# Two transformer passes: looped layers with phases, against one written-out pipeline with Wv and Wo joined

## The reference, cut to what matters

```python
for i in range(DEPTH):                      # 6
    x = attn_layer(shift_tokens(x), Wqkv[i], q_scale[i], k_scale[i], Wo[i]) + x
    x = ffn_layer(shift_tokens(x), ln_g[i], ln_b[i], W1[i], b1[i], W2[i], b2[i]) + x
```

## Time and profile before

| | us |
|---|---|
| median of three runs | 7947.51 (7939.41 to 7956.17) |
| span of the profiled execution | 7947.7 |
| TensorE busy (matmul) | 6508.3, 82% |
| DVE busy | 5680.7, 71% |
| ScalarE busy | 2813.2, 35% |
| GpSimd busy | 1991.7, 25% |

### The profile page before, as it was taken

The page is one execution under the profiler, slowest core; times in us unless marked ns, Lnnn a source line. Parts: engine busy times, 40 slices in busy tenths (PEclk is TensorE's granted clock), DMA queues, the critical chain, the costliest instruction groups (busy, mean ns, idle before and its releaser), DMA issues. The chain is left out here.

```text
span 7947.7 us, 238408 instructions
## 1 busy us (share of the span) xinstructions
PE 6508.3 (82%) x89716; PEld 4710.8 (59%) x89716; DVE 5680.7 (71%) x26551; ACT 2813.2 (35%) x7328; POOL 1991.7 (25%) x2075
## 2 busy tenths in 40 slices
PE   8999999999976666666666666679999999999887
PEld 5656656565656565655656565656565655656544
DVE  6676767676767777777777777777666676767566
ACT  4444444444432222222222222234444444444311
POOL 4343535353510000000000000034444353535200
PEclk9999999999975555555555555589999999999898
DMA  0000000000000000000000000000000000000000
GB/s 28 11 4 14 1 14 1 14 1 14 1 15 2 2 2 2 2 2 2 2 2 2 2 2 2 2 4 0 15 11 4 11 4 14 1 14 1 18 2 12
DMA packets 30765, 50.49 MB, mean 6 GB/s; under 512 B 2032, under 2 KB 25291, under 8 KB 28235
## 3 DMA queue, kind: packets, MB, share of 16 engines
q1 hardware_dynamic: 29614, 40.54, 1.6%
q10 hardware_dynamic: 412, 0.42, 0.0%
HBM read 39.91 MB, written 1.05 MB: 5 GB/s over the span
## 5 line engine op out<-in xcount | busy, mean ns | idle before, releaser
L1048 PE MATMUL g_bank<-hbuf,Wgates 128*128 128x2 f32 x2048 | 600.9, 363 | 1024.2 <-DVE hbuf L1136 970.3
L1048 PEld LDWEIGHTS g_bank<-hbuf,Wgates 128*128 128x128 f32 x2048 | 513.0, 311 | 1140.0 <-DVE hbuf L1136 1085.3
L1090 ACT ACTIVATE tg<-g_bank 128x2 f32<-128x2 f32 x1024 | 176.1, 172 | 1690.9 <-PE g_bank L1048 1690.9
L1156 POOL TENSOR_TENSOR xB<-hbuf,xA 128x32 f32 x64 | 16.4, 256 | 2853.0 <-DVE hbuf L1136 2853.0
L371 POOL TENSOR_TENSOR t1b<-t1b,t2b 128x1024 f32<-128x1024 f32 x192 | 451.7, 2354 | 687.1 <-DVE t2b L523 687.1
L371 POOL TENSOR_TENSOR t1a<-t1a,t2a 128x1024 f32<-128x1024 f32 x192 | 451.7, 2354 | 684.7 <-DVE t2a L523 684.7
L1060 PE MATMUL e_bank<-tg,Weg 128*128 128x2 f32 x2048 | 579.4, 352 | 0.0
L1032 PEld LDWEIGHTS s_bank<-hparts,Wparts 128*128 128x128 bf16 x12288 | 571.0, 117 | 0.0
L1110 DVE TENSOR_SCALAR sg<-es 128x4 f32<-128x4 f32 x1024 | 174.4, 170 | 554.5 <-ACT es L1092 554.5
L1060 PEld LDWEIGHTS e_bank<-tg,Weg 128*128 128x128 f32 x2048 | 515.1, 312 | 0.0
L1032 PE MATMUL s_bank<-hparts,Wparts 128*128 128x2 bf16 x12288 | 469.6, 165 | 0.0
(11 more groups left out here) (435 smaller groups left out, 16401.7 us busy)
## 6 DMA issues: line engine op xcount, KB each, us to landing
Wqkv<-in_L_ffn_Wqkv SPq DMA_DIRECT2D x13, 1536.0 KB, 6.5
Wo<-in_L_ffn_Wo SPq DMA_DIRECT2D x13, 512.0 KB, 7.6
W<-in_L_ffn_W SPq DMA_DIRECT2D x12, 341.0 KB
W<-in_L_ffn_W SPq DMA_DIRECT2D x12, 128.0 KB
xt<-in_L_attn_x SPq DMA_DIRECT2D x2, 512.0 KB
rope<-in_rope SPq DMA_DIRECT2D x1, 1024.0 KB, 7.5
out<-ot SPq DMA_DIRECT2D x4, 256.0 KB
W<-in_L_ffn_W SPq DMA_DIRECT2D x12, 42.5 KB
```

Source lines behind the costliest of these rows:

```text
L1048: pe.matmul(g_bank[j][:, s * B:(s + 1) * B], Wg[:, 3, 1, :], h, start=False, stop=True, skip_group_check=True).then_inc(g_done, 1)
L1090: act.activation(tg[:, :], g_bank[j][:, s * B:(s + 1) * B], ACT.Tanh).then_inc(tg_ready, 1)
```

## The change

layer_phase and FeedForward go. transformer now builds one program for each engine for all 96 tiles of a pass (six layers of 16), written out, with no loop on the device and no pause between layers. A tile passes through four iterations: project (new), turn and score (now), values and weighting (old; last). The feed-forward part runs in the same iterations, on groups of two tiles (256 tokens), spread over an even and an odd iteration.

- Wv and Wo are joined: for each head the product of its part of Wv and its part of Wo is a 128 x 128 matrix, made on TensorE once for a layer (turn_weights, join_weights, take_weights, keep_weights) during the layer before. The values of a head are then already 128 outputs wide, and the weighting (attend) sums over the heads into one 128 x 128 result; L440, L459, L593 and the copies L623 go, one transpose (turn_output) and a small copy (take_output) come.
- q and k share one pair of banks one after the other: project_k waits until DVE has read q, project_q of the next tile until it has read k. Values and turned probabilities share one bank (vp), the weighted output has one, feed-forward has two.
- Values take 16 matmuls a tile (32-column weights, 512 columns, four column groups); scores and weighting 32 matmuls each with 128-row, 32-column weights over 128 columns. The keys lie in KT with zeros in the rows of the other head.
- DVE subtracts the maximum in two halves of 512 columns, ScalarE takes one exponential over 1024 columns, DVE sums the rows over two axes; GpSimd multiplies the probabilities by the reciprocals (norm_probs, two halves) before they are turned.
- GpSimd also makes the rotation tables and moves the last 32 keys to the next tile's buffer (move_k).
- The statistics of the feed-forward part are made for every two tiles, with the twelve root steps each time (normalise).
- SyncE loads the weights of two layers ahead into double buffers; the first layer's weights are no longer loaded in load_phase but at the start of the pass.

```diff
-def layer_phase(nc, c, layer, nm):
...
+    def project_q(n):
+        layer = tile_place(n)[0]
+        pe.wait_ge(s.weights_in[layer % 2], 16 * (layer // 2 + 1))
+        pe.wait_ge(s.xq_ready, 2 * n + 2)
+        if n:
+            pe.wait_ge(s.k_prod, 2 * n)
+        for h in range(2):
+            last = pe.matmul(qk[h], c.xq[n % 4][:, :], c.Wqk[layer % 2][:, h * 512:(h + 1) * 512], start=True, stop=True)
+        last.then_inc(s.q_done, 1)
+    def project_k(n):
+        layer = tile_place(n)[0]
+        pe.wait_ge(s.q_prod, 2 * n + 2)
+        for h in range(2):
+            last = pe.matmul(qk[h], c.xq[n % 4][:, :], c.Wqk[layer % 2][:, INNER + h * 512:INNER + (h + 1) * 512], start=True, stop=True)
+        last.then_inc(s.k_done, 1)
...
+    def turn_q(n):
+        pe.wait_ge(s.q_scaled, n + 1)
+        if n:
+            pe.wait_ge(s.centred, 2 * n)
+        for half in range(2):
+            for k in range(half * HALF, (half + 1) * HALF):
+                last = pe.transpose(sc[:, k * P:(k + 1) * P], t1[:, k * P:(k + 1) * P], c.ident[:, :])
+            last.then_inc(s.q_turned, 1)
...
+    def score(n):
+            pe.matmul(sc[:, h * 512:(h + 1) * 512], c.identb[:, :], c.mask[:, t, :].unsqueeze(1).to_broadcast([P, 8, KEYS]),
+                      start=True, stop=False, skip_group_check=True)
+        for pair in range(PAIRS):
+            for w in range(NW):
+                last = pe.matmul(sc[WIN * w:WIN * w + WIN, pair * 2 * KEYS:(pair + 1) * 2 * KEYS],
+                                 c.QT[:, pair, WIN * w:WIN * w + WIN],
+                                 c.KT[n % 2][:, pair, :, WIN * w:WIN * w + KEYS],
+                                 start=False, stop=True, skip_group_check=True)
+        last.then_inc(s.scored, 1)
...
+    def values(n, w):
+        layer = tile_place(n)[0]
+        pe.wait_ge(s.wvo_ready, 4 * (layer + 1))
+        if w == 0 and n:
+            pe.wait_ge(s.v_ready, 4 * n)
+            before, j = divmod(n + 1, TILES)
+            if before + 1 < N // TILES and 6 <= j < 8:
+                pe.wait_ge(s.wv_ready, 2 * (before + 1) + j - 5)
+            if before + 1 < N // TILES and 8 <= j < 12:
+                pe.wait_ge(s.wvo_ready, 4 * (before + 1) + j - 7)
+        if w == 1 or w == 3:
+            pe.wait_ge(s.v_ready, 4 * n + w)
+        if w == 2:
+            pe.wait_ge(s.pt_ready, 2 * n + 2)
+        for hq in range(4):
+            last = pe.matmul(vp[WIN * hq:WIN * hq + WIN, :], c.xq[n % 4][:, WIN * w:WIN * w + WIN], c.Wvo[layer % 2][:, hq, :],
+                             start=True, stop=True)
+        last.then_inc(s.v_done, 1)
...
+    def attend(n):
+        pe.wait_ge(s.v_ready, 4 * n + 4)
+        pe.wait_ge(s.pt_ready, 2 * n + 2)
+        if n:
+            pe.wait_ge(s.x_done, n)
+        first = NW * (n % 2)
+        for pc in range(2):
+            for quad in range(QUADS):
+                for w in range(NW):
+                    slot = (first + w - 1 + pc) % (2 * NW)
+                    last = pe.matmul(o[WIN * w:WIN * w + WIN, 0:P], c.PT[:, pc, quad * P + WIN * w:quad * P + WIN * w + WIN],
+                                     c.Vw[:, slot, quad * P:(quad + 1) * P],
+                                     start=(pc == 0 and quad == 0), stop=(pc == 1 and quad == QUADS - 1), skip_group_check=True)
+        last.then_inc(s.pv_done, 1)
...
+    def join_weights(layer, hq):
+        pe.wait_ge(s.wv_ready, 2 * layer + 2)
+        if hq:
+            pe.wait_ge(s.wvo_ready, 4 * layer + hq)
+        par = hq % 2
+        rows = slice(64 * par, 64 * par + 64)
+        for quad in range(QUADS):
+            pair = 2 * quad + hq // 2
+            last = pe.matmul(vp[:, quad * P:(quad + 1) * P], c.WvT[rows, pair, :], c.Wo[rows, pair, :], start=True, stop=True)
+        last.then_inc(s.wvo_done, 1)
...
+    for i in range(N + 6):
+        new, now, old, last = i, i - 1, i - 2, i - 3
+        even, g = i % 2 == 0, (i - 4) // 2
+        layer, j = divmod(i, TILES)
+        if new < N:
+            project_q(new)
+        if 0 <= now < N:
+            turn_q(now)
+        if 0 <= last < N:
+            attend(last)
+        if 0 <= old < N:
+            values(old, 0)
+        if 0 <= now < N:
+            turn_k(now)
+        if 0 <= last < N:
+            turn_output(last)
+        if 0 <= old < N:
+            values(old, 1)
+        if even and 0 <= g - 1 < G:
+            lins(g - 1)
+        if not even and 0 <= g < G:
+            back(g)
+        if new < N:
+            project_k(new)
+        if 0 <= old < N:
+            turn_probs(old, 0)
+        if 0 <= now < N:
+            score(now)
+        if 0 <= old < N:
+            turn_probs(old, 1)
+            values(old, 2)
+        if even and 0 <= g - 1 < G:
+            contract(g - 1)
+        if not even and 0 <= g < G:
+            gates(g)
+        if 0 <= old < N:
+            values(old, 3)
+        if even and 0 <= g < G:
+            rows(g)
+        if layer + 1 < N // TILES and 6 <= j < 12:
+            pe.wait_ge(s.v_ready, 4 * (old + 1))
+            if j < 8:
+                turn_weights(layer + 1, j - 6)
+            else:
+                join_weights(layer + 1, j - 8)
...
+    def rotate_q(n):
+        dve.wait_ge(s.table, 4 * (tile_place(n)[0] + 1))
+        dve.wait_ge(s.q_sq, n + 1)
+        if n:
+            dve.wait_ge(s.q_turned, 2 * n)
+            dve.wait_ge(s.q_sum, n)
+        rotate(0, n, s.q_prod)
+    def rotate_k(n):
+        dve.wait_ge(s.k_sq, n + 1)
+        if n:
+            dve.wait_ge(s.k_turned, 2 * n)
+            dve.wait_ge(s.k_sum, n)
+        rotate(1, n, s.k_prod)
...
+    def norms(n):
+        dve.wait_ge(s.q_ssq, n + 1)
+        dve.wait_ge(s.k_ssq, n + 1)
+        if n:
+            dve.wait_ge(s.q_scaled, n)
+            dve.wait_ge(s.k_scaled, n)
+        rsqrt_steps(dve, s.newton, n * NEWTON, c.ssq[:, :], c.rnorm[:, :], c.ntmp[:, :], 1e-24, 0.0)
+    def largest(n):
+        dve.wait_ge(s.scored, n + 1)
+        dve.tensor_reduce(c.mx[:, :], sc.rearrange("p (h j) -> p h j", j=KEYS), AX.X, ALU.max).then_inc(s.max_done, 1)
+        dve.wait_ge(s.max_done, n + 1)
+        if n >= 2:
+            dve.wait_ge(s.p_turned, 2 * (n - 1))
+        for pc in range(2):
+            dve.tensor_tensor(c.probs[n % 2][:, :, pc, :, :],
+                              sc.rearrange("p (q h a j) -> p q h a j", h=4, a=2, j=WIN)[:, :, :, pc, :],
+                              c.mx[:, :].rearrange("p (q h) -> p q h", h=4).unsqueeze(3).to_broadcast([P, QUADS, 4, WIN]),
+                              ALU.subtract).then_inc(s.centred, 1)
+    def row_sums(n):
+        dve.wait_ge(s.exp_done, n + 1)
+        if n >= 2:
+            dve.wait_ge(s.inverted, n - 1)
+        dve.tensor_reduce(c.rsum[n % 2][:, :].rearrange("p (q h) -> p q h", h=4),
+                          c.probs[n % 2][:, :, :, :, :].rearrange("p q a h j -> p q h a j"), AX.XY, ALU.add).then_inc(s.summed, 1)
+    def invert(n):
+        dve.wait_ge(s.summed, n + 1)
+        if n >= 2:
+            dve.wait_ge(s.p_scaled, 2 * (n - 1))
+        dve.reciprocal(c.rinv[n % 2][:, :], c.rsum[n % 2][:, :]).then_inc(s.inverted, 1)
...
+    for i in range(N + 6):
+        new, now, old, last = i, i - 1, i - 2, i - 3
+        even, g = i % 2 == 0, (i - 4) // 2
+        if new < N:
+            rotate_q(new)
+            squares_q(new)
+        if 0 <= last < N:
+            residual(last)
+        if even and 0 <= g - 1 < G:
+            multiply(g - 1)
+        if new < N:
+            rotate_k(new)
+        if 0 <= now < N:
+            largest(now)
+        if even and 0 <= g - 1 < G:
+            finish(g - 1)
+        if new < N:
+            squares_k(new)
+            norms(new)
+        if 0 <= now < N:
+            row_sums(now)
+            invert(now)
+        if even and 0 <= g < G:
+            normalise(g)
...
+    def exponent(n):
+        act.wait_ge(s.centred, 2 * n + 2)
+        pr = c.probs[n % 2][:, :, :, :, :].rearrange("p q a h j -> p (q a h j)")
+        act.activation(pr, pr, ACT.Exp).then_inc(s.exp_done, 1)
...
+    def move_k(n):
+        if n:
+            pool.wait_ge(s.kt_ready, 4 * n)
+        if n >= 2:
+            pool.wait_ge(s.scored, n - 1)
+        for par in range(2):
+            rows = slice(64 * par, 64 * par + 64)
+            if n % NT == 0:
+                pool.memset(c.KT[n % 2][rows, :, par, 0:WIN], 0.0).then_inc(s.k_moved, 1)
+            else:
+                pool.tensor_copy(c.KT[n % 2][rows, :, par, 0:WIN], c.KT[1 - n % 2][rows, :, par, P:]).then_inc(s.k_moved, 1)
+            pool.wait_ge(s.k_moved, 2 * n + par + 1)
+    def add_q(n):
+        pool.wait_ge(s.q_prod, 2 * n + 2)
+        pool.tensor_tensor(t1[:, 0:INNER], t1[:, 0:INNER], t2[:, 0:INNER], ALU.add).then_inc(s.q_sum, 1)
+    def add_k(n):
+        pool.wait_ge(s.k_prod, 2 * n + 2)
+        pool.tensor_tensor(t1[:, INNER:], t1[:, INNER:], t2[:, INNER:], ALU.add).then_inc(s.k_sum, 1)
+    def norm_q(n):
```

(39 more changed lines are left out.)

929 lines of the change are left out of this document (399 added, 530 removed).

## The result

The changed kernel takes 8003.16 us (median; 7992.66 to 8008.73) against 7945.38 for the kernel before on the same chip: 1.0069 times as long, with an interval of 1.0055 to 1.0084. It is slower, as forecast, by 58 us where 144 were forecast. The profiled execution spans 8001.0 us, 53 more than the one of before.

A forecast was written before the change was run, and what follows sets the result against it. TensorE bound the old passes; a cross-engine chain would bound the new: 42.05 + lock 4.0 + clock 1.4 + waits 0.4, 47.8 us a pair. With ends, 2338 a pass against 2266, twice +72: 8092, said 8090, range 7650 to 8450.

The forecast's parts named there:

- The walk: Step-by-step timing of an even and an odd iteration from rotate_q, giving 42.05 us a pair before additions.
- The chain: Dependent steps across engines, not any engine's sum, set the period: even 24.7 us, odd 17.35.
- 0.4 for waits: Some eight further semaphore waits behind the last arrival, 0.05 us each, 0.4 a pair.
- The lock: Even iteration: GpSimd's SBUF work holds normalise's small DVE steps, 4.0 us a pair, with 4.4, 3.3 or 0 possible.
- The clock: TensorE drops to half clock after long waits, slowing odd project_k: 1.4 us a pair, bounds 0 and 3.4.
- Joined weights and tables at nothing: Joining weights in TensorE's waits, ScalarE's copies and GpSimd's table products were given no cost, having room.
- The ends: Per pass: first five iterations -21 us, first weights loaded and joined +20, six draining iterations +45.
- the first rival: Faster, neither SBUF contention nor half clock bites: pair 43.0 us, total 7632, deciding at 46.3 a pair; chance 0.24.
- lock yes, clock no: Rival with SBUF contention but TensorE at full speed: pair 46.4 us, pass 2271, total 7958; chance 0.1.
- The code written out for 96 tiles, put at nothing: Transformer passes written out instead of looped on the device, costed at zero.

The follow-up runs named there:

- experiment 3: Changed kernel with GpSimd's probability scaling moved behind move_k in the next iteration, and it and norm_k placed behind normalise's root steps: 7802.17 us, ratio 0.9812.
- experiment 4: Changed kernel plus an unused 1.2 us DVE sum in each even iteration, between reciprocal and normalise: 7998.35 us, ratio 1.0062.
- experiment 5: Changed kernel plus an unused 1.2 us DVE sum in each odd iteration, behind the reciprocal: 7992.73 us, ratio 1.0053.
- experiment 12: Changed kernel with ScalarE subtracting the maximum and summing rows in sixteen exponentials a tile, DVE's subtractions and row sums removed: 8120.54 us, ratio 1.0218.
- experiment 6: Changed kernel with useless matmuls filling TensorE's wait between project_q and turn_q: 8045.42 us, ratio 1.0113.
- experiment 7: Changed kernel with GpSimd's norm_q in two halves, turn_q waiting for each half: 8054.0 us, ratio 1.0126.
- experiment 8: Changed kernel with ScalarE's gelu ahead of the copy of the joined weights: 8011.31 us, ratio 1.0076.

## Why the forecast was right in sign and too large in size

The walk, step against step (times from rotate_q behind turn_q; the example iteration has 1.66 us of half-clock attend before project_k, taken off):

| even | forecast | trace |
|---|---|---|
| rotate_k ends | 11.4 | 11.3 |
| maximum and subtractions end | 14.0 | 13.8 |
| finish ends | 15.1 | 15.1 |
| root steps end | 19.05 | 18.9 |
| row sums, reciprocal end | 20.6 | 20.5 |
| normalise ends, no lock | 24.7 | 24.29 (experiment 3) |
| odd, all of it | 17.35 | 17.48 |

- *The chain: right.* No engine's sum sets the period, and the two iterations of different length are there. With its 0.4 for waits the forecast had 42.45 a pair, the trace has 24.29 + 17.48 = 41.77; the allowance for waits was not needed. Experiments 4, 5 and 12 show that DVE's sum is not the bound.
- *The lock: right in kind and place, 3.4 where I said 4.0.* The walk let it start at the copy at 21.4, let one step in for each GpSimd instruction, and end with GpSimd's queue; so it does. In a quiet even iteration norm_k, the two halves of norm_probs and the two copies of move_k hold one step each, to 1.73, 0.97, 0.97, 0.30 and 0.25 us instead of 0.16 or 0.17. That is 3.4 us more in all, the whole of 27.67 - 24.29. Only the lengths were off: the walk to 4.4 gave each half 1.2 us and each copy 0.6, and they take 1.0 and 0.4. I had chosen 4.0 "nearer to the upper end" against 3.3 for the case that only forms with two SBUF inputs are held. The reason for the choice was sound: copy and scalar forms are held (L679, L85, L86). That the measured 3.4 lies beside the 3.3 is chance. The rule of the Trainium skill ("SBUF — State Buffer", section "Who interferes with whom"), that these forms contend too and that the other side blocks fully, agrees with these rows.
- *The clock: right in kind, mostly wrong in place, 0.8 where I said 1.4.* This is the step that failed. I let TensorE wait from 17.6 to 21.1, then be cold, and still be cold at project_k of the odd iteration. It does wait 3.34 us there, but the attend directly behind it takes the whole loss (3.60 for 1.95), under cover of the held normalise, where it costs nothing, and project_k is back at 1.98. What costs is the shorter wait of 2.2 us at the end of the odd iteration: the attend behind it is on TensorE's way to project_k of the even iteration, which then takes 29.3 instead of 27.7, in 12 of 27 iterations (iterations 7 to 12 of every layer left out). Quiet pairs have 27.66 + 17.48 = 45.14, all pairs outside those iterations 45.92: 0.78. In the changed kernel the forecast's own place for it turned up only in iterations 9 and 11 of the five layers that join weights for the next one (and at the very start of the pass), where project_k takes 2.7 to 3.8 us (3.49 in the second row of L381 above); in experiments 6 and 7 it took most odd iterations.
- *Joined weights and tables at nothing: wrong by 0.4.* Iterations 9 and 11 of a layer take 19.4 instead of 17.5, and the even ones beside them (28.7, 27.8 and 27.3 against a mean of 28.4) give part of it back: all pairs 46.29, those without joins 45.92, so 0.37 a pair. I had said that both engines "have room" for the copies and the tables. But a rotation table holds one step of normalise more, 1.06 us in two even iterations of a layer, and behind the longer waits (1.93 us for normalise and 1.82 for rotate_q, for one of 1.31) project_k falls to half clock. In experiment 8 the odd iteration's share is this half clock alone. In the changed kernel it overlaps with the late gelu, and the iteration takes 19.7 whether project_k takes 2.69 or 3.68; how the 0.37 divides is not shown.
- *The ends: 44 us forecast, 69 measured, wrong the other way.* 48 x 46.29 = 2222 of 2290.5. The first rotate_q is at 59.87, 27 us after the pass begins, for 20 forecast: TensorE waits 9.62 us for Wo and joins four times at half clock.

```profile
40.85 1.12 PE L476 MATMUL banksa<-ident,Wva 128*128 128x128 f32 x4 [9.62 <-DMA Woa<-in_L_ffn_Wo]
...
44.50 2.07 PE L488 MATMUL banksa<-Woa,WvTa 64*128 64x128 f32 x8 [0.68 <-ACT WvTa L797]
...
54.92 3.78 PE L374 MATMUL banksa<-Wqk0a,xq0a 128*128 128x512 f32 x4
```

  The first iterations save 17 for 21, and from the last tile's rotate_q at 2246.38 to the residual at 2323.1 it is 77 us, 59 behind an odd iteration of 17.5, for 45. The last group's feed-forward runs alone, step after step.

Together: (47.8 - 46.29) x 48 = 72 less, 25 more, so 47 less a pass and 95 in both; 8092 - 95 = 7997, and the profiled span is 8001. The terms of the 1.5 are 0.7 (chain and waits), 0.6 (lock), 0.6 (clock), less 0.4 (joins). Three terms erred in one direction and by about the same amount, since each time I had gone to the dearer side of what the rows allowed. Of the three only the clock had its mechanism in the wrong place; the other two are terms of the wrong size.

The point from which the first rival decides was put at 46.3 a pair, and the pair is 46.29. With the 44 us of ends that I had allowed, the changed kernel would thus be as fast as the one before; the 25 us a pass that the ends took beyond that are the whole loss. So the nearness was not seen: the ends, which I gave one line, decided the sign. That the sign came out right was luck, since the terms that I had reasoned for it were too dear and one that I had hardly looked at was too cheap. Of the rivals none came true as told; "lock yes, clock no" (46.4) has the measured pair, by another sum.

The code written out for 96 tiles, put at nothing, shows no cost in the trace: the quiet odd iterations of pass a take 17.48 us in the first layer as in the last, the quiet even ones 27.66 to 27.68. No run tested it by itself.

What isn't shown: why the half clock falls behind one wait of 2.2 us and not behind the next (12 of 27) was not pursued, and the ends were read from the timeline alone, no run changes them.

## What to carry to other kernels

Where DVE's tiny steps on SBUF follow a result that GpSimd is also waiting for, they stand behind GpSimd's whole queue; look for copies of a few columns that take over 1 us, and put a wait into GpSimd's program so that its long instructions come behind the short chain. Here moving the scaling alone was worth 182 us and made the new kernel 1.7% faster than the old one. With norm_k moved too and TensorE kept busy through its wait it was 2.7%, and about 3% with the two small changes of experiments 7 and 8. Fill a wait of TensorE only when the wait behind it is gone or short (the fill lost 42 us with 1.82 us of wait left in front of project_k, and gained 41 with 1.17), and price the filling and draining of a pipeline with the same care as its steady pair when the steady pairs come out equal.

## What the runs showed of the hardware

- A 128x2 copy and a 128x2 tensor_scalar of DVE are held by a GpSimd multiplication until it ends (1.73 and 0.97 us for 0.17), and in experiment 12 a 128x16 tensor_scalar by an add for 1.36 us; sums over 1024 columns from SBUF and the statistics from PSUM beside the same GpSimd instructions are not (1.16, 0.43). A short GpSimd copy holds a step too, but only until its own end (0.30, 0.25). A short GpSimd memset holds a tensor_scalar (0.33), but not a scalar_tensor_tensor beside it (0.16, at 624.15 in the changed kernel).
- The half clock does not vanish when one wait is filled: it moves to the next (attend 3.62 to 1.95, project_k 1.98 to 2.67). Starting turn_q on the first half of norm_q, worth 0.3 us in a quiet odd iteration (experiment 7), moved the mean of the odd iterations by 0.9.
- Sixteen exponentials over 64 columns with a sum each (two instructions apiece in the trace) take 4.6 us, 0.29 from start to start, against 1.06 for one over 1024.
